# A narrow cross-attention worked in pairs of key tiles, and a last cross-attention that opens with three plain f32 value tiles

## What is computed

```python
x = x + _L2_xattn_ref(_layernorm(x, axis=-1), ctx_4096, ctx_4096, ..., mask_SxS2_bk0)
...
x = x + _L3_xattn_ref(_layernorm(x, axis=-1), ctx_4096, mask_1x1xSxS2_ff0, ...)

def _L2_xattn_ref(q, k, v, w_q, w_k, w_v, w_out, mask):     # 32 query heads of 16, 8 kv groups
    query, key, value = q @ w_q.T, k @ w_k.T, v @ w_v.T     # then split into heads and groups
    scores = jnp.einsum('bghnd,bgsd->bghns', query, key) / D_HEAD ** 0.5
    scores = jnp.where(mask, scores, jnp.finfo(scores.dtype).min)
    attention = jax.nn.softmax(scores, axis=-1)
    out = jnp.einsum('bghns,bgsd->bghnd', attention, value)
    return out.transpose(0, 3, 1, 2, 4).reshape(b, n, D_MODEL) @ w_out.T

def _L3_xattn_ref(hidden_states, cross_attention_states, attention_mask, ...):   # 32 heads of 128, 8 kv heads
    q, k, v = ... @ q_proj_w.T, ... @ k_proj_w.T, ... @ v_proj_w.T
    q, k = rmsnorm(q, q_norm_w), rmsnorm(k, k_norm_w)
    attn = jax.nn.softmax(jnp.einsum('bhqd,bhkd->bhqk', q, k) * scale + attention_mask, axis=-1)
    return jnp.einsum('bhqk,bhkd->bhqd', attn, v) ... @ o_proj_w.T
```

## Time and profile before

| | us |
|---|---|
| median of 3 runs | 1691.44 (1689.5 to 1693.83) |
| the profiled execution | 1685.28 |
| span of that execution | 1683.5 |
| L2x: from its first scores to its first turned score | 842.4 to 861.25 |
| L2x: loop over 8 groups | 861.25 to 1028.6 |
| L3x: opening, up to the k projection of group 0 | 1165.57 to 1226.93 |

### The profile page before, as it was taken

One profiled execution on the slowest core, in us unless ns is written; L12 is line 12 of the kernel. 1 busy time (PEld: TensorE's weight loads), 2 busy tenths in 40 slices (PEclk: granted clock), 3 DMA queues, 4 the chain that ended last, 5 costly groups with the idle time before them and its releaser, 6 DMA issues. The chain is left out here.

```text
span 1683.5 us, 23015 instructions
## 1 busy us (share of the span) xinstructions
PE 1562.3 (93%) x7457; PEld 1167.1 (69%) x7457; DVE 1044.1 (62%) x2136; ACT 889.3 (53%) x1624; POOL 324.6 (19%) x280
## 2 busy tenths in 40 slices
PE   4999999999999988998989996997999999999986
PEld 4788778778775443487566664785777787777864
DVE  5666666675665882275478883664157667676663
ACT  4545554554554451264148884552266667666661
POOL 0000000000001340054136663450011011111110
PEclk9999999999999999999999998998999999999999
DMA  7011011011019107262362212536311122211012
GB/s 259 27 38 57 30 37 62 25 58 42 25 54 364 43 24 266 99 194 97 100 153 29 33 20 87 170 122 231 113 61 53 44 81 80 76 56 56 25 58 79
DMA packets 57282, 148.52 MB, mean 88 GB/s; under 512 B 5969, under 2 KB 28113, under 8 KB 48129
## 3 DMA queue, kind: packets, MB, share of 16 engines
q1 hardware_dynamic: 57216, 147.72, 26.8%
HBM read 133.55 MB, written 8.65 MB: 84 GB/s over the span
## 5 line engine op out<-in xcount | busy, mean ns | idle before, releaser
L1288 DVE TENSOR_TENSOR L3x_k_lo<-bank,L3x_k_hi 128x512 fp32r<-128x512 f32 x128 | 86.0, 687 | 52.2 <-ACT L3x_k_hi L1177 51.9
L2488 POOL TENSOR_TENSOR L2x_p_lo<-L2x_e_t,L2x_p_hi 128x512 fp32r<-128x512 f32 x80 | 105.3, 1326 | 63.0 <-ACT L2x_p_hi L2673 62.4
L664 DVE TENSOR_TENSOR L0x_k_lo<-bank,L0x_k_hi 128x512 fp32r<-128x512 f32 x128 | 85.7, 688 | 42.5 <-ACT L0x_k_hi L577 42.1
L376 PE MATMUL bank<-L0x_ctx_hi,L0x_w_hi 128*128 128x512 f32 x256 | 103.7, 405 | 4.2 <-DVE L0x_ctx_lo L603 4.2
L577 ACT ACTIVATE L0x_k_hi<-bank 128x512 fp32r<-128x512 f32 x128 | 74.2, 599 | 54.7 <-PE bank L482 54.7
L378 PE MATMUL bank<-L0x_ctx_hi,L0x_w_lo 128*128 128x512 f32 x256 | 101.0, 395 | 0.0
L886 POOL TENSOR_TENSOR L3x_v_lo<-L3x_v_raw,L3x_v_hi 128x512 fp32r<-128x512 f32 x32 | 40.5, 1302 | 310.2 <-ACT L3x_v_hi L1168 310.2
L377 PE MATMUL bank<-L0x_ctx_lo,L0x_w_hi 128*128 128x512 f32 x256 | 100.2, 391 | 0.0
L2716 DVE CUSTOM_DVE_ANT_0 L2x_junk<-bank,L2x_mask 128x512 f32<-128x512 f32 x128 | 85.1, 688 | 20.2 <-PE bank L2574 10.8
L1177 ACT ACTIVATE L3x_k_hi<-bank 128x512 fp32r<-128x512 f32 x128 | 74.1, 604 | 41.6 <-PE bank L1046 41.2
L336 POOL TENSOR_TENSOR L0x_r_hi<-L0x_r_sum,ones 128x4 fp32r<-128x4 f32 x8 | 1.6, 203 | 484.2 <-DVE L0x_r_sum L668 484.2
(11 more groups left out here) (630 smaller groups left out, 4388.3 us busy)
## 6 DMA issues: line engine op xcount, KB each, us to landing
L0x_w_kqv<-in_L0x_kqv SPq DMA_DIRECT2D x7, 1536.0 KB, 6.3
L0x_w_o<-in_L0x_o SPq DMA_DIRECT2D x8, 1024.0 KB, 4.8
L1a_w_o<-in_L1a_o SPq DMA_DIRECT2D x8, 1024.0 KB, 7.7
L2a_w_o<-in_L2a_o SPq DMA_DIRECT2D x8, 1024.0 KB, 7.2
L3x_w_q<-in_L3x_kq SPq DMA_DIRECT2D x8, 1024.0 KB, 5.4
L3x_w_o<-in_L3x_o SPq DMA_DIRECT2D x8, 1024.0 KB, 4.8
L3x_v_raw<-L3x_values SPq DMA_DIRECT2D x8, 1024.0 KB, 4.8
L0x_s<-in_ctx_t SPq DMA_DIRECT2D x4, 1024.0 KB, 12.1
```

The source lines that it names most:

```text
L376: pe.matmul(out, left[0], right[0], start=start, stop=False)
L664: dve.tensor_tensor(p_lo[:, kt % 4, :], ring_bank(kt)[:], bits(p_hi[:, kt % 4, :]), ALU.subtract).then_inc(p_ready, 1)
L1288: dve.tensor_tensor(p_lo[:, kt % 4, :], ring_bank(kt)[:], bits(p_hi[:, kt % 4, :]), ALU.subtract).then_inc(p_ready, 1)
L2488: pool.tensor_tensor(p_lo[:, t % 8, :], e_of(t), bits(p_hi[:, t % 8, :]), ALU.subtract).then_inc(low_pool, 1)
```

## The change

In L2x the tiles are worked in pairs: exponential, rounding, low half and score maximum become operations of 128x1024 over two neighbouring banks, for which the eight banks become one PSUM tensor. The exponential always goes to SBUF, to one of three buffers of two tiles, and its rounding stands directly behind it. POOL makes the low half of pairs 0, 2, 3, 4 and 6 of a group (none in the last), DVE that of pairs 1, 5 and 7 from SBUF. Values are weighed three pairs later. The scores no longer belong to one group ahead: they are made at an iteration's end up to twelve pairs ahead of it, through one pair of banks, 4 and 5 (and banks 2 and 3 too, by turns, ahead of the loop). The spread goes to the output bank of its group, at the seventh pair. ACT copies the values, after the second pair.

In L3x PE begins with value tile 0 as plain f32 matmuls on the context and weights as loaded, then the four transposes, then tiles 1 and 2 in the same way, without the dummy matmuls; the waits for the splits stand ahead of tile 3. There are four tile buffers, all in v_raw, the q projection and the sum of squares stand after tiles 3 and 8, the weight loads are issued ahead of the ninth store, and the load of the first values comes behind all stores. The diff's core:

```diff
-        v_tile = (o_t, rinv)
+        v_tile = [v_raw[:, 4 * b:4 * b + 4, :] for b in range(4)]
...
-                load_v(0)
-                load_k_weights(1)
-                load_q_weights(1)
                 for i in range(KT):
+                    if i == 8:
+                        load_k_weights(1)
+                        load_q_weights(1)
                     sp.wait_ge(tile_kept, i + 1)
                     sp.dma_start(values.place(KT + i),
-                                 v_tile[i % 2][:].rearrange("p (g d) -> p g d", g=HG)).then_inc(tile_stored[i % 2], 16)
-                for b in range(2):
-                    sp.wait_ge(tile_stored[b], KT // 2 * 16)
+                                 v_tile[i % 4]).then_inc(tile_stored[i % 4], 16)
+                for b in range(4):
+                    sp.wait_ge(tile_stored[b], KT // 4 * 16)
+                load_v(0)
...
-                norm.keep_clock(pe)
-                norm.tensor(pe)
...
-                    if kt % 4 == 0:
-                        pe.wait_ge(ctx_kept, kt // 4 + 1)
                     if kt >= 4:
                         pe.wait_ge(tile_kept, kt - 3)
                     for c in range(CT):
+                        if kt < PLAIN:
+                            mm = pe.matmul(ring_bank(kt)[:], s_sb[:, c, keys], w_v[:, c, :], start=(c == 0),
+                                           stop=(c == CT - 1))
+                            continue
...
-                    if first:
-                        pe.wait_ge(tile_kept, KT)
-                    else:
+                    if not first:
                         pe.wait_ge(p_ready, g * 16)
                     for n in range(NC):
+                        if first:
+                            pe.wait_ge(tile_kept, KT - 3 + n)
...
-                pe.wait_ge(wv_kept, 1)
+                pe.wait_ge(w_v_in, 16)
+                pe.wait_ge(ctx_in[0], 16)
                 for kt in range(KT):
+                    if kt == PLAIN:
+                        pe.wait_ge(wv_kept, 1)
+                    if kt >= PLAIN and (kt == PLAIN or kt % 4 == 0):
+                        pe.wait_ge(ctx_kept, kt // 4 + 1)
                     project_values(kt)
-                    if kt == 2:
+                    if kt == 0:
+                        norm.tensor(pe)
+                    if kt == 3:
                         project_q(0)
-                    if kt == 5:
+                    if kt == 8:
                         sum_q_squares(0, used=False)
...
+                def split_context(n):
                     act.wait_ge(ctx_in[n], 16)
                     act.activation(ctx_hi[:, :, chunk(n)], s_sb[:, :, chunk(n)], ACT.Copy).then_inc(ctx_hi_kept, 1)
+
+                def keep_tile(i):
+                    act.wait_ge(tile_filled, i + 1)
+                    if i >= 4:
+                        act.wait_ge(tile_stored[i % 4], i // 4 * 16)
+                    act.activation(v_tile[i % 4], ring_bank(i)[:].rearrange("p (g d) -> p g d", g=HG),
+                                   ACT.Copy).then_inc(tile_kept, 1)
+
+                split_context(0)
+                split_context(1)
+                keep_tile(0)
+                keep_tile(1)
+                split_context(2)
+                keep_tile(2)
+                split_context(3)
                 split_w(0)
+                for i in range(3, KT):
+                    keep_tile(i)
+                    if i == 4:
                         square_q(0)
-                    if i == 6:
+                    if i == 9:
                         log_q(0)
                         root_q(0)
-                    if i == 8:
+                    if i == 11:
                         keep_q_hi(0)
...
-    LAG = 5
+    PAIRS = KT // 2
+    LAG = 3
+    AHEAD = 12
...
+    POOL_PAIRS = (0, 2, 3, 4, 6)
...
-        st_bank = lambda t: core.bank[t % 4]
-        s_bank = lambda n: core.bank[4 + n % 2]
+        st_bank = lambda u, k: core.bank[2 * (u % 2) + k]
+        s_pair = lambda m: 2 if m % 2 and m < PAIRS else 4
+        pair = lambda b: core.banks[:, b * 512:(b + 2) * 512]
...
+        by_pool = lambda u: u < (NG - 1) * PAIRS and u % PAIRS in POOL_PAIRS
+        scored = lambda u: PAIRS + 2 if u < 0 else min(NG * PAIRS, u + AHEAD + 1, PAIRS + 3 + 2 * u)
+        p_at = lambda u: slice(2 * (u % 4), 2 * (u % 4) + 2)
...
+                def score(m):
...
+                    if m >= PAIRS:
+                        pe.wait_ge(s_read, m)
+                    elif m >= 2:
+                        pe.wait_ge(s_read, m - 1)
+                    for k in range(2):
+                        c = 2 * (i % 2) + k
+                        mm = pe.matmul(core.bank[s_pair(m) + k][:], q_sc[g % 2][:, i // 2 * P:(i // 2 + 1) * P],
+                                       k_st[g % 3][:, c * 512:(c + 1) * 512], start=True, stop=True)
+                    mm.then_inc(s_ready, 1)
...
-                    pe.matmul(core.bank[4][:], core.ones[:], diag[:].rearrange("p h q -> p (h q)"),
+                    if g >= 2:
+                        pe.wait_ge(o_kept, g - 1)
+                    pe.matmul(out_bank(g)[:], core.ones[:], diag[:].rearrange("p h q -> p (h q)"),
...
+                for m in range(PAIRS):
+                    score(m)
+                    project_v(2 + m // 4, m % 4)
+                score(PAIRS)
                 spread_max(0)
+                score(PAIRS + 1)
                 pe.wait_ge(lo_kept, 2 * NC + 1)
                 pe.wait_ge(mask_ready, 2)
+                for u in range(NG * PAIRS + LAG):
+                    if u < NG * PAIRS:
+                        turned_scores(u)
+                    if u % PAIRS == PAIRS - 2 and u // PAIRS + 1 < NG:
+                        spread_max(u // PAIRS + 1)
+                    if u >= LAG:
+                        weigh(u - LAG)
+                    for m in range(scored(u - 1), scored(u)):
+                        score(m)
...
+                def exponential(u):
+                    act.wait_ge(st_ready, u + 1)
+                    if u >= 3:
+                        wait_low(act, u - 3)
+                    act.activation(e_t[u % 3][:].rearrange("p k n -> p (k n)"), pair(2 * (u % 2)),
+                                   ACT.Exp).then_inc(exp_done, 1)
+
+                def round_p(u):
+                    act.wait_ge(exp_done, u + 1)
+                    if u >= 4:
+                        act.wait_ge(pv_done, u - 3)
+                    act.activation(p_hi[:, p_at(u), :], e_t[u % 3][:], ACT.Copy).then_inc(hi_ready, 1)
+
+                def keep_v(g):
+                    if g >= 2:
+                        act.wait_ge(pv_done, (g - 1) * PAIRS)
+                    to = v_st[g % 2][:, 0:KT * VW].rearrange("p (k d) -> p k d", d=VW)
+                    for half, v in enumerate((v_hi, v_lo)):
+                        copy = act.activation(to[:, :, half * E:(half + 1) * E], bits(v[:, :, g * E:(g + 1) * E]),
+                                              ACT.Copy)
+                    copy.then_inc(v_kept, 1)
...
+                for u in range(NG * PAIRS):
+                    g, i = u // PAIRS, u % PAIRS
+                    if i == PAIRS - 1 and g + 1 < NG:
                         keep_max(g + 1)
+                    exponential(u)
+                    round_p(u)
+                    if u == 0:
+                        act.wait_ge(lo_kept, 2 * NC + 1)
+                        keep_v(0)
+                    if i == 1 and g > 0:
+                        keep_v(g)
+                    if i == LAG and g > 0:
...
+                def take_max(m):
...
+                    at = slice(i % 2 * 1024, i % 2 * 1024 + 1024)
+                    dve.tensor_tensor_reduce(junk[:], pair(s_pair(m)), bits(mask_sb[:, at]), 1.0, LOWEST, ALU.add,
+                                             ALU.max, part_max[:, i // 2, i % 2:i % 2 + 1]).then_inc(s_read, 1)
...
+                def low_half(u):
+                    if 0 <= u < NG * PAIRS and not by_pool(u):
+                        dve.wait_ge(hi_ready, u + 1)
+                        dve.tensor_tensor(p_lo[:, p_at(u), :], e_t[u % 3][:], bits(p_hi[:, p_at(u), :]),
                                           ALU.subtract).then_inc(low_dve, 1)
...
+                for m in range(PAIRS):
+                    take_max(m)
+                    if m == 5:
                         split_v(2)
                 take_row_max(0)
                 split_v(3)
+                take_max(PAIRS)
                 keep_max(0)
...
+                for u in range(NG * PAIRS + 1):
+                    g, i = u // PAIRS, u % PAIRS
+                    for m in range(scored(u - 2), scored(u - 1)):
+                        take_max(m)
+                        if m % PAIRS == PAIRS - 1:
+                            take_row_max(m // PAIRS)
+                    low_half(u - 1)
+                    if i == PAIRS - 1 and g + 1 < NG:
+                        keep_max(g + 1)
...
```

(13 more changed lines are left out.)

174 lines of the change are left out of this document (41 added, 133 removed).

## The result

The changed kernel takes 1678.68 us in the median of 4 runs (1676.68 to 1680.89), against 1690.47 us for the kernel before: ratio 0.9927, 95% interval 0.9911 to 0.9944. Measured a second time, in 9 runs beside 20 of before, the ratio is 0.9951 (0.9934 to 0.9967). So the gain is 8 to 12 us by the ratios, 6.5 to 11.8 by the medians, and the forecast of 1679.8 lies on the first median. The second measurement, with more runs, speaks for the lower end, and the trace says that the sum behind the forecast came out for partly wrong reasons.

What follows compares the result with a forecast made beforehand. TensorE, busy 93% of the span, was taken to bound the kernel. L3x opening -9.1, L2x ahead of its loop -2.6 and L2x loop 0.0 sum to -11.7: 1691.44 - 11.7 = 1679.8 us, range 1669 to 1691.

Steps and rivals of the forecast that it cites:

- L3x opening, -9.1: Start of L3x to k projection: three plain f32 tiles cover the 5.28-us split wait; 52.3 us against 61.36.
- the copy that was counted exposed: L3x opening: the 0.69-us copy freeing the transposes' bank, counted as uncovered though other banks might cover it.
- L2x ahead of the loop, -2.6: Before L2x's loop: eight 1024-wide row-max operations replace sixteen of 512; 2.6 us saved, ends -4 and -1.
- L2x loop, 0.0: L2x's loop: 167.4 us against 167.35, scattered waits saved but largely given back; within about -8 and +8.
- The start: First four pairs of L2x's loop: five score pairs at a 2.22-us chain step, 13.2 us instead of 9.3.
- The five groups: Ordinary L2x groups: 20.86 us each, 104.3 in all, including a 1.2-us PE stall behind the diagonal.
- The last twelve pairs: End of L2x's loop, without scores: ACT leads at 1.95 us a pair; 29.0 us in all.
- B: L2x loop: the diagonal's wait for POOL is covered, 7.8 us less, so -19.5 in total, 1672; chance 0.18.
- E: L2x: wide operations on PSUM cost twice the narrow, chain 2.39, ACT 2.2 a pair; +6, 1686; chance 0.10.
- Rival C: L2x loop: DVE's low halves collide with POOL's, about 2.2 us lost in seven groups or more; 1695; chance 0.12.
- Rival D: L3x opening: plain tiles run at clock 0.50, 10.3 us of tiles taking twice as long; 1690; chance 0.05.
- The total, 1679.8: Whole kernel: the summed -11.7 us put on the median of 1691.44; this main forecast had chance 0.52.

## Why the prediction was right, and where it was not

- **L3x opening, -9.1: right**, and by its terms. The sum of 52.3 us was 52.30 (52.29 to 52.31 in seven profiles with this opening and no dummies); the copy that was counted exposed is the 0.78 idle; three tiles are what covers the splits (two wait, four overpay), and the split into 3.0 for the buffers and 5.9 for the tiles was shown by leaving the tiles out. The load of the first values, moved behind the stores, held nothing up: the group behind it took 51.5 us as before.
- **L2x ahead of the loop, -2.6: right in kind**, 2.2 measured. The wide maximum costs 1.22, and 0.08 more for the read of its accumulator; the sum had 1.23 for both, estimated from the wide subtract.
- **L2x loop, 0.0: wrong, by 4.3 to 4.9 us.** This is the step that failed, and it is a matter of sizes in three of its terms. The start was put at 13.2 us for four pairs and took 14.3, or 16.4 with the clock's fall: six score pairs are made there, not five (one, two, two and one in the first four iterations, by the program's own rule), and a step of the chain is 2.31 us (863.36, 865.67, 867.98 in the starts of the scores), not 2.22, most of it by the accumulator's read. The five groups were put at 20.86 and took 21.13 to 21.56: the stall behind the diagonal is 1.4 instead of 1.2, and PE waits some 0.3 us for the copied maximum at each group's start, where 0.13 was allowed. The last twelve pairs took 29.9 instead of 29.0 (30.6 in the second profile): ACT leads there as forecast, but with a step of 2.01 us for 1.95. The mechanism of the group (the diagonal waits out POOL's doubled subtract and holds the scores) was as forecast, and two runs that remove the wait in different ways bear it out: the diagonal on ACT in full, POOL's pairs moved in part. The Trainium skill, "SBUF — State Buffer", section "Who interferes with whom", has the rule; this case's 0.69 with POOL idle and 2.38 behind a 2.41-us POOL operation agree with it.
- **Rivals B and E**: the diagonal's wait was not covered, groups took 21.1 and not B's 19.6. Of E, the chain's step of 2.31 lies halfway to its 2.39, but the wide maximum is 1.22 where twice the narrow one is 1.38, and ACT's step 2.01 where E has 2.2.
- **Rival C did not come about**: 29 low halves on DVE with both operands in SBUF have a median of 1.22 us, with one at 2.18, at the end of the seventh group; those of POOL lie at 2.36 to 2.87, median 2.41. The point from which it decides, 2.95, was not reached.
- **Rival D**, the low clock in the plain tiles, did not happen: 1.00 from 1165.8 to 1230. But its mechanism struck elsewhere, at L2x's thin start and in L3x's last group, places that the forecast never looked at.
- **The total, 1679.8 against 1678.7 and 1681.7: right by luck in part.** The sum was put on 1691.44, the median of three runs of the kernel before; seventeen and twenty later runs have 1687.9 and 1688.1. On 1688.1 the same sum gives 1676.4, 5 us under the 1681.7 measured beside it, which is about the loop's +4.9 that the sum did not have. In the two profiled executions the gain is 6.6 us and not 11.7: the loop, the last group and L1x with L1a lost 10.1, and two stages that nobody touched gave back 5.7. These two, L2a and L2f, took 123.4 and 123.5 us in the profiles with the old L2x; in eleven with the new one, 117 to 120 eight times and 123.5 three times, though the code up to there was the same in four of the eight and in all three. In all five profiles of 123.4 and more POOL's subtract went ahead of DVE's operation in L2a. Whether the change makes these stages shorter is open.

## What to carry to other kernels

Work that a later operation needs only as a split can start as plain f32 on the unsplit data, if the plain form's extra price (0.63 us a tile here) is less than the wait it covers; count how many tiles the wait is long, since one fewer waits again and one more overpays. When operations are made twice as wide, look for whoever waits for an operation of another engine: its wait grows too (the diagonal from 1.64 to 2.38 us, 0.69 without POOL). The way out here was another engine, which POOL's subtracts did not hold up (ACT, 0.39 us a copy beside them), more than a new place in the same queue. A pipeline that runs further ahead has to be filled once: each step of its chain that PE can't cover at the start is paid in full. One pair less ahead shortened the loop by 4.2 us in its one profile; the times do not show it.

## What the runs showed of the hardware

The granted clock fell in several places behind stretches in which PE waited for part of the time; it stayed low for some 3 to 10 us, and a fall cost 1.2 to 3.4 us in a stage that was otherwise equal: 1.2 and 2.4 in the last group of L3x, 1.7 in L1x, 3.4 in L2f. Of the same thin stretch some executions fell and some did not: the last group of L3x took 55.2 us at 1.00 and 57.7 at 0.94 with the same 235 matmuls. The Trainium skill, "TensorE: Matmul & The Clock Gate", section "HAM oscillation — how this bites in real kernels", tells that waits between stretches of matmuls bring the low clock back; the start of L2x agrees (0.50 there, 1.00 when filled), while the last group shows that the same wait can pass without a fall.

Where a DVE operation with two operands in SBUF and a POOL subtract begin together, one of them waited for the other here, and which one changed from execution to execution. In L1a and in L2a the two begin within 0.03 us of each other in all thirteen profiles, and the code of these stages is the same in all. In six profiles of L1a and six of L2a DVE's operation took 0.69 us and POOL's 1.8; in the other seven of each POOL's took 1.3 and DVE's 1.8 to 1.9, and PE's next work on the tile came 1.1 us later.

For a change of half a per cent such falls and waits are as large as the terms of the sum, so that a forecast that is good to 0.1 us in its own stage is still uncertain by about 5 us in the total.
